# A fused AdaLN block (time mixing, channel mixing, mixture of experts) on one core: the hand-over from the shared experts to the routed experts in another order

## The reference, cut to what matters

```python
sh_mid = gelu(einsum('th,ehd->ted', xt, Wsh_up))          # 2 shared experts, 512 -> 2 x 256
shared_out = einsum('ted,edh->th', sh_mid, Wsh_down)
probs = softmax(xt @ W_router)
top_v, top_i = top_k(probs, 2)
rt_mid = gelu(einsum('th,ehd->ted', xt, Wrt_up))          # 16 routed experts
routed_out = einsum('ted,edh->th', rt_mid * gate[:, :, None], Wrt_down)
...
x = x + gb * (shared_out + routed_out)
```

## Time and profile before

| | |
|---|---|
| runs before, us | 958.32, 965.66, 972.61 (median 965.66) |
| the profiled execution, us | 972.61 |
| its span, first to last instruction, us | 970.9 |
| mean granted TensorE clock, share of full | 0.969 |
| busy share of the span: PE, DVE, ACT, POOL | 93%, 55%, 40%, 39% |
| shared experts' hand-over to the loop, us from the start | about 727 to 742 |
| loop over routed tiles, us from the start | about 742 to 901 |

### The profile page before, as it was taken

The page is one execution under the profiler, slowest core; times in us unless marked ns, Lnnn a source line. Parts: engine busy times, 40 slices in busy tenths (PEclk is TensorE's granted clock), DMA queues, the critical chain, the costliest instruction groups (busy, mean ns, idle before and its releaser), DMA issues.

```text
span 970.9 us, 13509 instructions
## 1 busy us (share of the span) xinstructions
PE 902.5 (93%) x4264; PEld 726.8 (75%) x4265; DVE 537.3 (55%) x983; ACT 383.7 (40%) x632; POOL 382.2 (39%) x279
## 2 busy tenths in 40 slices
PE   7898779999998999999999899999999998999983
PEld 2457658878776888887888788878878887888762
DVE  5896998997747111445153515351864443444558
ACT  2566465573735533221132113234542332333431
POOL 2332200100022447136004600468347699893553
PEclk9898989999998999999999999999999998999987
DMA  9548478565064426153016301663545787776556
GB/s 357 183 134 276 138 227 259 165 207 184 12 201 148 157 91 206 55 184 120 22 55 210 114 1 55 216 236 123 167 148 176 254 272 241 237 251 228 171 184 205
DMA packets 105632, 166.69 MB, mean 172 GB/s; under 512 B 8152, under 2 KB 53208, under 8 KB 102512
## 3 DMA queue, kind: packets, MB, share of 16 engines
q1 hardware_dynamic: 59472, 112.59, 34.3%
q0 software_dynamic: 8960, 34.61, 11.3%
q10 hardware_dynamic: 37152, 18.88, 6.6%
HBM read 98.63 MB, written 67.42 MB: 171 GB/s over the span
## 4 chain that ended last, share of the span: by engine, by line
PE 72%; DVE 15%; DMA 5%; issue 4%; ACT 2%; SPq 1%; DVEq 0%; ACTq 0%
PE kk_ps L420 6%; PE kk_ps L422 6%; PE kv_ps L420 6%; PE kk_ps L421 6%; PE kv_ps L422 6%; PE kv_ps L421 6%; PE mm_ps L420 4%; PE mm_ps L421 4%; PE mm_ps L422 4%; PE up_ps L420 3%; PE dn_ps L420 3%; PE dn_ps L422 3%; PE dn_ps L421 3%; PE up_ps L421 3%; PE up_ps L422 3%
## 5 line engine op out<-in xcount | busy, mean ns | idle before, releaser
L1533 DVE TENSOR_TENSOR silu<-kk_ps,silu 128x512 fp32r<-128x512 f32 x64 | 44.3, 692 | 207.8 <-ACT silu L2137 193.1
L2133 ACT ACTIVATE kk_ps<-kk_ps 128x512 f32<-128x512 f32 x64 | 37.2, 582 | 212.7 <-PE kk_ps L422 208.3
L420 PE MATMUL kk_ps<-xk,cm_w 128*128 128x512 f32 x256 | 101.6, 397 | 0.0
L420 PE MATMUL kv_ps<-cm_w,silu 128*128 128x512 f32 x256 | 100.6, 393 | 0.0
L422 PE MATMUL kk_ps<-xk,cm_w 128*128 128x512 f32 x256 | 100.2, 392 | 0.0
L421 PE MATMUL kk_ps<-xk,cm_w 128*128 128x512 f32 x256 | 100.2, 391 | 0.0
L422 PE MATMUL kv_ps<-cm_w,silu 128*128 128x512 f32 x256 | 99.7, 390 | 0.0
L421 PE MATMUL kv_ps<-cm_w,silu 128*128 128x512 f32 x256 | 99.6, 389 | 0.0
L2307 POOL TENSOR_TENSOR rs<-mv,neghalf 128x4 f32<-128x4 f32 x12 | 13.6, 1135 | 160.8 <-DVE mv L1262 160.7
L2300 POOL TENSOR_TENSOR cm_w<-stage,cm_w 128x1024 fp32r<-128x1024 f32 x16 | 38.6, 2423 | 91.3 <-ACT cm_w L1924 91.3
L1823 DVE TENSOR_TENSOR xsT<-xs_ps,xsT 128x512 fp32r<-128x512 f32 x42 | 29.0, 692 | 79.1 <-ACT xsT L2216 79.1
(11 more groups left out here) (276 smaller groups left out, 2367.5 us busy)
## 6 DMA issues: line engine op xcount, KB each, us to landing
xs_s<-zero ACTq DMA_DIRECT2D x13, 1024.0 KB, 6.1
xsb<-xs_s SPq DMA_DIRECT2D x44, 256.0 KB, 3.4
ys_s<-ysb SPq DMA_DIRECT2D x41, 256.0 KB, 3.3
ex_raw<-in_wex POOLq DMA_DIRECT2D x9, 1024.0 KB
stage<-in_wcm SPq DMA_DIRECT2D x16, 512.0 KB, 3.9
wmod<-in_wmod SPq DMA_DIRECT2D x6, 1024.0 KB, 13.6
ex_raw<-in_wex SPq DMA_DIRECT2D x6, 1024.0 KB, 5.8
stage<-in_wtm SPq DMA_DIRECT2D x10, 512.0 KB, 6.5
```

Of the source, the lines that this page charges most:

```text
L420: pe.matmul(out, lhs[0], rhs[0], start=first, stop=False)
L1533: dve.tensor_tensor(silu[:, g % NSILU, 1, :], kk_ps[g % 2][:, :], silu[:, g % NSILU, 0, :].bitcast(F32), ALU.subtract).then_inc(s_silo, 1)
L2133: act.activation(kk_ps[g % 2][:, :], kk_ps[g % 2][:, :], ACT.Silu).then_inc(s_silu, 1)
```

## The change

PE's stream around the start of the loop is written in another order, DVE's, ACT's and POOL's with it:

- PE does the first tile's `turn_x(0)` one shared tile earlier, then the shared tile 2, then `up` of the first tile, then `turn_x(1)`, then the whole shared tile 3. The scalar loads of the first two table words stand behind shared tile 2, that of `pairs` behind everything, just before the loop. A wait for the eighth `gb_shared` stands on PE before the loop; before, DVE made `down` wait for it through the count `s_y4`.
- DVE does `gb_shared(TT + 2)` after `turned_lo(0, 1)`; ACT does the first `gelu4` before the second `turned_hi`.
- POOL starts the load of expert `PRE` (4) without waiting for the first two loads of `xsb`, splits it before `ht_lo(2)`, and issues all eight `base_add` in a row behind `ht_lo(2)`; before, two stood behind each of four later `expert_split`.

```diff
@@ PE
             shared_down(1, [0], every)
-            shared_down(1, [1, 2], every)
+            shared_down(1, [1], every)
             pe.wait_ge(s_tab, 1)
...
+            turn_x(0, 16)
+            shared_down(1, [2], every)
             w0 = word_of(0)
             w1 = word_of(1)
-            kept = [nc.alloc_register(mybir.EngineType.PE, f"kept_word{k}") for k in range(2)]
-            nc.reg_mov(kept[0], w0)
-            nc.reg_mov(kept[1], w1)
-            pairs = pe.value_load(tend[0:1, NE:NE + 1], min_val=NE // 2, max_val=NS // 2)
-            turn_x(0, 16)
-            turn_x(1, 16)
-            shared_down(1, [3], first)
             pe.wait_ge(s_gsh, SB * TT - 2)
             up(w0, slot_of(w0), 0, 1)
-            shared_down(1, [3], rest)
+            turn_x(1, 16)
+            shared_down(1, [3], every)
             pe.wait_ge(s_gsh, SB * TT - 1)
             turn_m(0, 1)
+            pe.wait_ge(s_gsh, SB * TT)
...
+            kept = [nc.alloc_register(mybir.EngineType.PE, f"kept_word{k}") for k in range(2)]
+            nc.reg_mov(kept[0], w0)
+            nc.reg_mov(kept[1], w1)
+            pairs = pe.value_load(tend[0:1, NE:NE + 1], min_val=NE // 2, max_val=NS // 2)
             with pe.Fori(0, pairs) as i:
@@ DVE
             gb_shared(TT + 1)
-            gb_shared(TT + 2)
...
+            dve.sem_inc(s_y4, AHEAD)
             dve.sem_inc(s_yst[1], 16)
             dve.sem_inc(s_yst[0], 16)
             turned_lo(0, 1)
+            gb_shared(TT + 2)
             turned_lo(1, 2)
             gb_shared(TT + 3)
-            dve.wait_ge(s_gsh, SB * TT)
-            dve.sem_inc(s_y4, AHEAD)
             turned_mid_lo(0, 1)
@@ ACT
             turned_hi(0, 1)
+            gelu4(0, 1)
             turned_hi(1, 2)
-            gelu4(0, 1)
             turned_mid_hi(0, 1)
@@ POOL
+            expert_load(PRE)
             pool.wait_ge(s_wlo, 38)
             pool.sem_inc(s_exr, 8 * PRE - 1)
             pool.wait_ge(s_tab, 1)
-            for par in range(2):
-                pool.wait_ge(s_xs[par], 16)
-            expert_load(PRE)
+            expert_split(PRE)
             ht_lo(2)
-            expert_split(PRE)
+            for t in range(SB * TT):
+                base_add(t)
             expert_load(PRE + 1)
 
             for e in range(PRE + 1, NE):
                 if e + 1 < NE:
                     expert_load(e + 1)
                 expert_split(e)
-                if e <= PRE + TT:
-                    base_add(2 * (e - PRE - 1))
-                    base_add(2 * (e - PRE - 1) + 1)
```

## The result

| | before | after |
|---|---|---|
| median of 20 runs, us | 965.50 | 970.28 |
| lowest and highest, us | 957.79 to 975.75 | 964.87 to 976.11 |
| the profiled execution and its span, us | 972.61, 970.9 | 967.75, 966.0 |

The ratio of after to before is 1.0081, with a 95% interval of 1.0058 to 1.0104: slower by 5.6 to 10.0 us, and far inside 2%. (The plain difference of the two medians is smaller, 4.8 us.) The forecast was 969.7 us in a range of 957 to 979. The two profiled executions alone say the opposite (966.0 against 970.9 us of span): the hand-over of after is 7.9 us longer and its loop 4.5 us shorter, but what decides is the stretch behind the loop, 64.8 us from the last transposes of `xsb` to the end against 73.2, whose instructions the change leaves alone. So this case is also one about how much a single profile can carry.

A forecast was written before the change was run, and what follows sets the result against it. TensorE, busy 93% of the span, was taken as the bound, so only holes in its stream count. Hand-over + 5.4, additions saved - 4.4 and their burst + 3.0 made + 4.0 on 965.66: 969.7 us, range 957 to 979.

The forecast's parts named there:

- The first transposes: PE before `turn_x(0)`: the `xsb` load lands late beside the 1 MB expert load; +2.7 us, ends 0.1 and 3.7.
- The clock behind it: PE after the hole before the first transposes: a slow clock costs +1.3 us, range 0 to 2.7.
- The entry: PE before the loop: the `gb_shared` wait, scalar load and branch delay `up` by 1.4 us, range 0.9 to 1.6.
- The hand-over: PE from the shared tiles into the loop: late first transposes, slow clock and loop entry together cost +5.4 us.
- The additions saved: Loop, 770 to 821 us: waits vanish with the `base_add` pairs; 7.4 us in the profiled execution, 4.4 for the median.
- The burst: Loop behind the eight additions in a row: one 1.5 us wait and half a clock fall, +3.0 us, ends 0 and 11.
- The sum: Whole kernel: + 5.4 - 4.4 + 3.0 = + 4.0 us on 965.66, giving 969.7 us, no change with a lean to slower.
- The cheap hand-over: Rival, chance 0.26: first `xsb` load slips ahead of the 1 MB, additions' packets don't block; 962.8 us, or 959.8.
- The starving burst: Rival, chance 0.12: in the loop the additions hold the DMA engines, PE waits 8.4 us; + 17.8, or 983 us.
- the waits come from the expert loads and remain: Rival, chance 0.06: loop waits come from expert loads, not additions, and stay; hand-over costs 1.5, giving 967 us.

The follow-up runs named there:

- after_masked: Control: after with only PE's wait on `s_exr` written as `word & 127`; 970.30 us, ratio to before 1.0038 to 1.0100.
- order_only: After with POOL's stream of before (late 1 MB load, additions in pairs); 965.62 us, ratio to before 1.0035 to 1.0077.
- late_load: After with POOL again waiting for the first two `xsb` loads before loading expert 4; 967.91 us, ratio to before 1.0069 to 1.0103.
- burst: Before with only the eight additions moved, in a row behind the split of expert 4; 966.49 us, ratio to before 1.0046 to 1.0087.
- entry_back: After with the wait for the eighth `gb_shared` back on DVE and scalar loads behind shared tile 2; 967.28 us, ratio to before 1.0003 to 1.0072.
- no_adds: Before without the eight additions and the wait for them, so the output lacks one summand; 965.43 us, ratio to before 0.9994 to 1.0050.
- before_masked: Control: before with only PE's wait on `s_exr` written as `word & 127`; 961.51 us, ratio to before 0.9950 to 1.0003.
- early_load: Before with only the 1 MB load of expert 4 moved ahead of the waits for `xsb`; 963.30 us, ratio to before 1.0033 to 1.0067.
- spread_all: Before with one addition behind each of eight splits and one `gb` load behind each of the last four; 967.97 us, ratio 1.0024 to 1.0073.

## Why the prediction came out as it did

**The first transposes.** Right in cause and release, and near in size: predicted a hole of 2.7 us, with 3.7 as the dear end; measured 3.34, 3.38 and 3.45, and once 1.54. I had the right row and counted it from the wrong end. The load of the earlier trace rows took 4.9 us from its own issue, a microsecond behind the 1 MB, but 5.9 from the start of the 1 MB, and it is the latter that repeats. Put behind 730.55 it gives 736.45, a hole of 3.3 us. I had also written that by the packet rule of the Trainium skill the hole would be well under 2.7. That took an equal share of packets for an equal share of the engines; with packets of 8 and 2 KB the share was 79 to 21, and with that share the rule agrees with the long hole.

**The clock behind it.** Predicted 1.3, range 0 to 2.7. What H of after holds beyond its two holes is 7.9 - 3.34 - 1.92 = 2.6 us; in after_masked, 7.1 - 3.45 - 2.04 = 1.6. Both lie in the range and above the value that I took.

**The entry.** Predicted 1.4, range 0.9 to 1.6; measured holes of 1.92, 1.99 and 2.04. Outside the range, by 0.3 to 0.4 us. Behind `gb_shared` I counted 0.2 + 0.49 + 0.43 = 1.1 us, and the chain shows 1.40. And `gb_shared` now ends 0.51 us behind PE's transposes (747.50 + 0.69 against 747.30 + 0.38), where I had reckoned with 0.30 (741.88 against 741.58). The two make the missing 0.5 us. A term for the clock behind this hole I left out without a reason, though I had one for the first: it was 0 in after and after_masked, but 1.6 us in order_only and 1.3 in late_load.

**The hand-over** in all: predicted 5.4, measured 7.9 in after and 7.1 in after_masked.

**The additions saved.** Here the prediction failed in size: "I take the middle, 4.4". With the pairs in their old place four other profiles lose 0.9 to 1.5 us in that stretch, not 4.4. I had seen that the execution lay 6.95 us above the median and that its long wait might be a thing of that run alone. Then I averaged instead of taking the low end of 1.3, which is where the usual run lies.

**The burst.** Predicted 3.0, made of one wait of 1.5 us and half a fall of the clock. Measured 3.3 to 5.3, from several late turns. The clock, which I had counted at half a fall, didn't fall in the burst of after, of burst, of late_load or of entry_back (1.00 from 755 to 782 us, and in after behind both waits), so the 3.0 is near the low end of what was measured for half the wrong reason.

**The sum.** With the measured terms: hand-over +7.1 to 7.9, additions -0.9 to -1.5 saved and +3.3 to 5.3 paid, in all +8.9 to +12.3 us. The ratio says +5.6 to +10.0, the controls on one chip 970.30 - 961.51 = +8.8. The forecast of +4.0 had the right sign and the right parts, and lies below the interval: 3 us too much were saved, about 2 us too little paid at the hand-over, and up to 2 us too little for the burst. The median came out only 0.6 us from the predicted time, since the plain medians differ by 4.8 us; that is luck, and closer than the working deserves. Two sums of the prediction are off besides: eleven turns of 3.735 are 41.09 us, not 41.06, and the ends of its terms give 959 to 983 us, where it says 960 to 977.

**The rivals.** The cheap hand-over fell with the first hole. The starving burst fell too: no hole of after, burst or late_load there passed 1.9 us, where the rival needed 8.4. In packets it wasn't so far off, as q1 had 767 against 1212. That the waits come from the expert loads and remain fell with no_adds, whose B is 0, and its price for the hand-over, 1.5 us, with H. But what it would have meant for the additions, that moving them saves next to nothing, is near to what the runs show.

**What stays open.** The tail behind the loop differs from one profiled execution to the next (64.8 to 73.2 us from the last transposes of `xsb` to the end), by as much as the effects here. PE's timeline in the tail of before, and that of before_masked:

```profile
923.38 0.39 PE L421 MATMUL dn_ps<-ex_w,mid 128*128 128x512 f32 x1 [1.05 <-issue]
925.53 0.39 PE L422 MATMUL dn_ps<-ex_w,mid 128*128 128x512 f32 x1 [1.77 <-issue]
```

```profile
914.77 0.39 PE L422 MATMUL dn_ps<-ex_w,mid 128*128 128x512 f32 x1 [1.14 <-issue]
916.94 0.42 PE L421 MATMUL dn_ps<-ex_w,mid 128*128 128x512 f32 x1 [1.04 <-issue]
```

The profiled execution of after has no such hole, the one of after_masked has four of 0.5 to 1.04 us. What PE waits for there the profile doesn't name, and no run was made to find out. Open is also why early_load and order_only are 5 us slower than the runs of before beside them, though their H and the clock at the entry explain 1.6 and some 4 us. Part of it may be the low median of those runs, 959.35 against 963.48 in the next group; that isn't shown.

## What to carry to other kernels

A hole is the landing of a transfer less the arrival of the engine that needs it: pulling the consumer forward (a hole of 0.21 us) and letting a big transfer in front of the loads (1.25) were each cheap and dear together (3.34), so cost them as a pair, and count the landing from the start of the transfer in front. A scalar load cost nothing under queued matmuls here and 0.73 us behind a wait; keep waits and register loads off the entry of a loop on the busy engine, and let an engine with slack hold the wait. And before counting a stall as something to save, look whether it stands in more than one execution: one profile that lies 7 us above the median shows what can go wrong, not what usually does.

## What I had not expected of the hardware

- A load of 256 KB on q1, issued 0.3 us behind a load of 1 MB on q0, took 5.7 us; issued 1.0 us behind it, 4.9; issued 2.1 us behind it, 3.9 us; alone, 2.5 us. All three landed 5.9 to 6.0 us behind the start of the 1 MB. In the first, both queues had the same number of packets (100 and 98 in 2.5 us), of 8 and of 2 KB.
- Idle stretches of PE of 3.34 to 3.45 us were followed by the 1.2 GHz level each time, but for times that cost 2.6 us once and 1.6 us another time. Around 2 us both happened: it fell behind 1.89 us (spread_all) and twice behind 1.99 us (order_only, late_load), and stayed at 1.00 behind 1.87 (burst), 1.92 (after) and 2.04 us (after_masked).
- The same eight additions of 256 KB landed in 9.7 us (median) when issued in a row, and in 4.3 us when issued one by one.
